# Expert-row scatters over 128 partitions instead of 125, with three spare rows each

## What is computed

```python
h = _layernorm(x)
msg = h[src] + relvectors[edge_type_16]
red = jax.ops.segment_sum(msg, dst, num_segments=6250)
x = x + _gru_cell(red, h, w_ih, w_hh, b_ih, b_hh)

n = _layernorm(x)
gate_scores = n @ Wg + bg                       # 8 experts
_, idx = jax.lax.top_k(gate_scores, 2)          # each row goes to two experts
mf = one_hot(idx, 8).sum(-2)
h = gelu(einsum('td,edh->teh', n, W1) + b1, approximate=False)   # 256 -> 512
y = einsum('teh,ehd->ted', h, W2) + b2                           # 512 -> 256
x = x + einsum('ted,te->td', y, mf)
```

## Time and profile before

| | |
|---|---|
| median of three runs | 1831.66 us (1830.85 to 1835.15) |
| the profiled execution: its time | 1842.09 us |
| its span, first to last instruction | 1839.3 us |
| busy share PE / DVE / ACT / POOL | 76% / 55% / 40% / 53% |
| granted TensorE clock, mean | 0.86 of full speed |
| scatters (line 689) | 100, 125.9 us busy on POOL |
| gathers (line 680) | 648, 665.5 us busy on POOL |

### The profile page before, as it was taken

How to read it: one execution, slowest core, us unless ns; L and a number is a source line. 1 busy time by engine, 2 the same in 40 slices (tenths; PEclk the granted TensorE clock), 3 DMA queues, 4 the chain that set the end, 5 groups by cost and what they waited for, 6 DMA issues and landing times. The chain is left out here.

```text
span 1839.3 us, 36012 instructions
## 1 busy us (share of the span) xinstructions
PE 1398.4 (76%) x12887; PEld 1115.1 (61%) x12887; DVE 1018.0 (55%) x2768; ACT 744.5 (40%) x1613; POOL 978.4 (53%) x868
## 2 busy tenths in 40 slices
PE   1347888888888887777788887776655579999992
PEld 1224556666666666555666666665445469999992
DVE  8735555365565554555566665576333555555551
ACT  6223334343343443444333332222112257766661
POOL 2365555465555564654665655666564235555552
PEclk8569989889989998888899888896876789999996
DMA  9644423243333343432333433333347145555556
GB/s 304 174 128 152 133 75 101 89 117 110 102 99 103 96 113 105 118 107 70 104 114 113 118 109 101 97 93 92 94 122 245 44 99 100 96 94 95 93 88 162
DMA packets 132377, 209.97 MB, mean 114 GB/s; under 512 B 26552, under 2 KB 99837, under 8 KB 130919
## 3 DMA queue, kind: packets, MB, share of 16 engines
q0 software_dynamic: 60032, 112.63, 25.3%
q1 hardware_dynamic: 72167, 94.97, 17.5%
HBM read 158.70 MB, written 57.76 MB: 118 GB/s over the span
## 5 line engine op out<-in xcount | busy, mean ns | idle before, releaser
L680 POOL DMA_INDIRECT ring<-h_table,idx x648 | 665.5, 1027 | 537.1 <-PE P L1612 307.2
L793 ACT ACTIVATE amat<-P 128x300 f16<-128x300 f32 (+4 forms) x688 | 267.4, 438 | 506.5 <-PE P L1666 278.7
L1679 PE MATMUL P<-hs,amat 128*126 128x512 f16 (+4 forms) x1568 | 432.6, 413 | 0.6 <-issue 0.5
L1661 PE MATMUL P<-cone,lone 128*128 128x294 f16 (+4 forms) x920 | 194.4, 310 | 139.1 <-ACT amat L793 82.1
L734 POOL DMA_INDIRECT out_rows<-yo,xrows x112 | 177.6, 1586 | 160.9 <-DVE yo L1549 110.8
L1679 PEld LDWEIGHTS P<-hs,amat 128*126 128x126 f16 (+4 forms) x1568 | 193.0, 137 | 108.9 <-issue 30.6
L1661 PEld LDWEIGHTS P<-cone,lone 128*128 128x128 f16 x920 | 81.1, 105 | 213.8 <-ACT amat L793 109.5
L689 POOL DMA_INDIRECT expert_rows<-xrow,slots x100 | 125.9, 1259 | 121.2 <-DVE slots L1292 95.3
L1149 DVE TENSOR_TENSOR cone<-src_t,twice 128x1176 f16<-128x1176 f16 (+4 forms) x230 | 164.4, 715 | 0.0
L1893 PE MATMUL P<-xh,w_all 128*128 128x256 f16 x896 | 157.1, 274 | 0.0
L1540 DVE SCALAR_TENSOR_TENSOR gl<-gT,scales,gh 128x512 f16<-128x512 f32 x112 | 84.2, 752 | 126.9 <-ACT gh L917 126.0
(11 more groups left out here) (243 smaller groups left out, 2811.7 us busy)
## 6 DMA issues: line engine op xcount, KB each, us to landing
raw<-in_L_ffn_W_dram SPq DMA_DIRECT2D x32, 512.0 KB
xrows<-expert_rows SPq DMA_DIRECT2D x56, 257.0 KB, 3.1
ring<-h_table,idx POOLq DMA_INDIRECT x648
w_parts<-parts SPq DMA_DIRECT2D x16, 512.0 KB
w_all<-w_parts SPq DMA_DIRECT2D x8, 1024.0 KB
h_in<-h_table SPq DMA_DIRECT2D x25, 250.0 KB
x<-in_x_dram SPq DMA_DIRECT2D x25, 250.0 KB
out_rows<-x SPq DMA_DIRECT2D x25, 250.0 KB
```

What stands on the lines that cost most here:

```text
L680: nc.gpsimd.indirect_dma_start(out=ring[:, r, j, :], out_offset=None, in_=h_dram, in_offset=bass.IndirectOffsetOnAxis(ap=idx[:, slot, g * ...
L793: nc.scalar.activation(amat[:, b % 2, :, s * aw:(s + 1) * aw], P[2 + g % 2][:, 0:HIS * aw].rearrange("p (h w) -> p h w", w=aw), ACT.Copy). ...
L1661: nc.tensor.matmul(P[2 + g % 2][:, 0:HI * aw], src_of[:, m, :, t], dst_of[:, m, :, t], start=(n == 0), stop=(n == k - 1)).then_inc(a_used, 1)
L1679: nc.tensor.matmul(both, amat[:, b % 2, hi, 0:used], hs[:, hi, :], start=(hi == 0), stop=False)
```

## The change

`xrow` and `slots` grow from 125 to 128 partitions, so that each scatter moves 128 rows. The list store `expert_rows` gets 1024 more rows at its end (`SPARE`). At the start DVE fills partitions 96 to 127 of `xrow` with zeros and writes a spare place into every row of all eight columns of `slots`, a different one for each. The work per tile then overwrites the first 125 partitions of both; the places of partitions 125 to 127 stay, so the three further rows of a scatter go to spare rows that nobody reads. Nine instructions on DVE, before the tiles begin, are all that is added; no instruction of another engine is added, taken away or moved, and the order of the old ones is the same.

```diff
+SPARE = 8 * 128
...
-    xs_dram = nc.dram_tensor("expert_rows", [NE * RS + TB, D + 1], F32).ap()
+    xs_dram = nc.dram_tensor("expert_rows", [NE * RS + TB + SPARE, D + 1], F32).ap()
...
-        xrow = sb("xrow", [SUB, 2, 2, D + 1])
+        xrow = sb("xrow", [128, 2, 2, D + 1])
...
-        slots = sb("slots", [SUB, 2, 4], I32)
+        slots = sb("slots", [128, 2, 4], I32)
...
                 nc.vector.memset(ones3[:, :], 1.0)
+                nc.vector.memset(xrow[96:128, :, :, :], 0.0)
+                for n in range(8):
+                    ins = nc.vector.tensor_scalar(slots[:, n // 4, n % 4:n % 4 + 1], tok[:, 0:1], float(NE * RS + TB + 128 * n), None, ALU.add)
+                link(ins)
                 nc.vector.tensor_copy(carry[:, :], rowc[:, 0:NE])
...
-                nc.vector.tensor_scalar(xrow[:, i % 2, :, D:D + 1].bitcast(I32), tok[0:SUB, :].unsqueeze(2), float(T * t), None, ALU.add)
+                nc.vector.tensor_scalar(xrow[0:SUB, i % 2, :, D:D + 1].bitcast(I32), tok[0:SUB, :].unsqueeze(2), float(T * t), None, ALU.add)
...
-                nc.vector.tensor_copy(slots[:, i % 2, :], slot_f[:, :]).then_inc(slots_ready, 1)
+                nc.vector.tensor_copy(slots[0:SUB, i % 2, :], slot_f[:, :]).then_inc(slots_ready, 1)
```

More of the change, by code:

```diff
@@ L1254, in second_norm @@
                 link(nc.vector.reciprocal(rstd[0:SUB, 0, 0:2], std[0:SUB, 0, 0:2]))
-                nc.vector.tensor_scalar(xrow[:, i % 2, :, D:D + 1].bitcast(I32), tok[0:SUB, :].unsqueeze(2), float(T * t), None, ALU.add)
+                nc.vector.tensor_scalar(xrow[0:SUB, i % 2, :, D:D + 1].bitcast(I32), tok[0:SUB, :].unsqueeze(2), float(T * t), None, ALU.add)
                 for j in range(2):
-                    ins = nc.vector.tensor_scalar(xrow[:, i % 2, j, 0:D], x1[:, j, :], mv[0:SUB, 0, j, 0:1], rstd[0:SUB, 0, j:j + 1],
+                    ins = nc.vector.tensor_scalar(xrow[0:SUB, i % 2, j, 0:D], x1[:, j, :], mv[0:SUB, 0, j, 0:1], rstd[0:SUB, 0, j:j + 1],
                                                   ALU.subtract, ALU.mult)
@@ L1749, in transpose_x2 @@
                         at = k * T + j * SUB
-                        ins = nc.tensor.transpose(P[5][:, at:at + SUB], xrow[:, i % 2, j, k * 128:(k + 1) * 128], ident[0:SUB, 0:SUB])
+                        ins = nc.tensor.transpose(P[5][:, at:at + SUB], xrow[0:SUB, i % 2, j, k * 128:(k + 1) * 128], ident[0:SUB, 0:SUB])
                 ins.then_inc(x2_trans, 1)
```

## The result

The changed kernel is slower. Its median is 1876.3 us (1871.6 to 1878.7, four runs) beside 1833.4 us (1830.9 to 1849.1, four runs) of the kernel before: ratio 1.022, 95% interval 1.018 to 1.026. The profiled execution took 1874.92 us with a span of 1871.9, that of before 1842.09 with 1839.3. The lost time is some 43 us by the medians and 33 us by the two profiled executions. In these it lies in the graph stage: the matmuls of PE's sums start between 89.0 and 1427.0 us before (line 1612) and between 87.8 and 1458.5 us after (line 1617), 32.7 us more. PE's own work is not slower: 1398.4 us busy before and 1390.0 after, at mean granted clocks of 0.860 and 0.853.

What follows compares the result with a forecast made beforehand. PE was taken to bound the kernel, with POOL following it in the graph stage. +0.8 at the start, 0 in the graph stage and -0.4 at the change of stages gave +0.4, 1832.1 us unprofiled; range 1822 to 1842 us.

Steps and rivals of the forecast that it cites:

- What bounds the kernel: PE sets the expert stage; in the graph stage POOL follows PE, so time POOL saves there becomes idle time.
- The scatter's shape and POOL's time: Each scatter goes from 128 packets to 48, like a gather; POOL saves 16 us, nothing on the path.
- The start: Nine more DVE instructions in `small_weights`, 1.65 us together; bounds 0 and +1.65, taken as +0.8 us.
- The graph stage: PE's stalls before the sums (line 1612) while POOL's DMAs move data, 19.5 us before; change taken as 0.
- the gather row: Stretch 383 to 387 us with only gathers on the software queue, where PE stalls 2.6 us in four pieces.
- The bound of 19.5 us: Graph stage: all 19.5 us of PE's "issue" stalls before the sums gone, or as much again on top.
- The third one, slower: Scatters on all sixteen DMA engines stall PE more at line 1612; 1851.6 us if doubled, 1842 with half; chance 0.13.
- The second rival: Faster: long chains on few DMA engines cause PE's stalls; 1812.6 us if all go, 1822 with half; chance 0.17.
- The change of stages: SP's wait for the last scatter ends earlier, then DVE's table binds; bounds -0.47 and +1.6, taken as -0.4 us.
- The expert stage: No scatter of this kind, PE fills it, and the larger list store's added 1 MB is not read: 0.

## Why the prediction was wrong

- **What bounds the kernel.** That POOL follows PE, and that time POOL saves turns into its idle time, was right (350.2 us). The inference from it was wrong: an engine for which nobody waits can still slow another one. The table of waits has no row for that, only "remote" and "issue", whose rows at `amat` and line 1661 the prediction did not read.
- **The scatter's shape and POOL's time.** Right in the shape: 8000 packets fewer. POOL's time came out at -18 us for -16 forecast, in part by luck: the sum set the median scatter (1.19 us) against the mean gather (1.03). Mean against mean, 1.26 against 1.03 us, would have made it -23.
- **The start.** The added fill took 0.92 us and the eight instructions 0.6 us. PE's keys came at 82.81 us for 80.74. But DVE's first sum behind the stand, at 100.50 before, came at 93.83: the stand did not hang on these instructions. With 125 rows the additions cost 1.002. A loss of 0.8 us is too small to be seen in that; the additions are not the cause. The rows are the two groups of DVE (busy time, mean ns), then timelines of PE and DVE.

```profile
L1045 DVE MEMSET xrow<- 32x1028 f32 x1 | 0.9, 915 | 0.3 <-issue 0.3
L1047 DVE TENSOR_SCALAR slots<-cols 128x1 int32<-128x1 f32 x8 | 0.6, 145 | 0.0
...
82.81 3.11 PE L1788 MATMUL P<-group_f,to_slots 32*128 32x1 f32 x14 [11.08 <-DVE group_f L1127]
...
93.83 0.26 DVE L1119 TENSOR_TENSOR acc<-P,acc 128x96 f32 x1 [4.47 <-remote]
```

- **The graph stage: the step that failed.** "I take 0, the value of the gather row, the nearest to what the scatter becomes." The term was taken from PE's pauses at one line, and the gather row was read as a price that scatters would share either way. The runs show that the shape has a price of its own: 128 rows cost 1.022 and 1.029, 125 rows with all else of the change 1.002. The table of runs shows where: PE is held 7.5 us in a run of four scatters and eight gathers before, and 12.2 after. The term measured some +43 us by the medians, 32.7 between the first and the last sum of the profiled executions, and not 0. The bound of 19.5 us was too small, since it counted only the pauses before the sums, and those fell to 15.9 us.
- **The rivals.** The third one, slower, named the sixteen engines, and fourteen or sixteen engines do cost what five did not. Its place was wrong (the pauses before the sums), and its price less than half the real one. Its reason, packets that meet what PE needs from memory, is not borne out: SP's copies cost at most 1%, and rows of 4 bytes in a quarter of the packets cost as much as whole rows. The second rival, that long chains on few engines stall PE, was the wrong way round at this place.
- **The change of stages.** Right: SP's last wait there was for DVE's table, as this row of its waits in 1480 to 1530 us shows.

```profile
SPq L655 <- DVE tab L1510: 1.6, 1, 1.6
```

- **The expert stage.** Right: from the last of the graph sums to the end 412 us before and 413 after.

What is shown is that the shape costs the time, that its price depends on the place, that neither the bytes nor SP's weight traffic carry it, and that in one job a pause in the middle of each step takes it away. That runs of POOL's DMAs hold PE the longer, the longer they are, is what the traces show in those kernels; as a forecast of times it failed in three of the six kernels with pauses, and in a fourth POOL became the bound. That the 125-row form is cheap because it leaves eleven engines' share of those first microseconds unused is an argument from the table of runs; no run took it apart. By what path POOL's DMAs hold PE stays open.

## What to carry to other kernels

Look at what an engine does to others even where no wait names it: compare the observed semaphore updates with the records that should have made them, by what else was running. Where one engine issues many software DMAs in a row, a wait that breaks the row can be worth more than the time it costs (3% here in one job, nothing with more such waits in another), and a shorter instruction in the row is not by itself a gain. A small change to such a row should be judged with its neighbours, at more than one place.

## What was not expected of the hardware

- PE's semaphore updates came up to 16.6 us after its records while POOL's software DMAs ran without a break, and within 0.02 us when nothing moved; ACT's and DVE's came within 0.013 us throughout.
- The price does not go by the bytes: 1.5 us for each added scatter of 125 rows with 1028 bytes a row, 1.7 us with 4 bytes a row. The same 0.51 MB a tile on SP's queue gave a ratio of 1.002 (0.994 to 1.010).
- In the hold of before around 451 us, PE advanced by two matmuls every 0.72 us (451.30, 452.04, 452.75 us above).
- The same kernel's median moved between 1833 and 1903 us from job to job, which is more than the change itself.
